# Feed-forward input rows split by GpSimd and transposed by the DMA engines, in place of TensorE

## What is computed

```python
def ffn(x):                                  # k0, k1, k2 are booleans, read as +1 / -1
    h = concatenate([x, -x], -1)
    h = relu(s0 * (h @ sign(k0))) * 2        # 256 -> 512
    h = relu(s1 * (h @ sign(k1))) * 2        # 512 -> 512
    return s2 * (h @ sign(k2))               # 512 -> 128
x = x + 0.5 * ffn(layernorm(x))
x = x + attention(layernorm(x))              # 16 heads of 8; adds its input, then a layernorm with gamma, beta
x = x + 0.5 * ffn(layernorm(x))
```

## Time and profile before

| | before |
|---|---|
| median of 3 runs | 745.43 us |
| profiled execution | 745.53 us |
| its span | 743.7 us |
| outside the span | 1.8 us |
| one full iteration | 42.7 us |
| instructions in the span | 18698 |

### The profile page before, as it was taken

One profiled execution on the slowest core, in us unless ns is written; L12 is line 12 of the kernel. 1 busy time (PEld: TensorE's weight loads), 2 busy tenths in 40 slices (PEclk: granted clock), 3 DMA queues, 4 the chain that ended last, 5 costly groups with the idle time before them and its releaser, 6 DMA issues.

```text
span 743.7 us, 18698 instructions
## 1 busy us (share of the span) xinstructions
PE 695.9 (94%) x7347; PEld 336.0 (45%) x7347; DVE 649.1 (87%) x1270; ACT 510.4 (69%) x745; POOL 365.9 (49%) x650
## 2 busy tenths in 40 slices
PE   7878999999999999999999999999999998787887
PEld 3434344544444454444444444444445444342346
DVE  6687898989999899999989898999989898887766
ACT  3426777777777777777787777767777776766644
POOL 6532455574454647454463746445465745254330
PEclk9999999999999999999999999999999999999999
DMA  3101010201102020201102020110201001010000
GB/s 82 57 15 52 16 53 2 65 17 45 37 3 66 17 66 16 67 17 29 39 16 66 16 66 17 44 38 2 67 17 65 17 33 36 30 38 2 11 7 30
DMA packets 29527, 25.65 MB, mean 34 GB/s; under 512 B 4353, under 2 KB 29441, under 8 KB 29441
## 3 DMA queue, kind: packets, MB, share of 16 engines
q1 hardware_dynamic: 27824, 23.74, 10.0%
q10 hardware_dynamic: 1616, 0.72, 0.3%
HBM read 5.05 MB, written 4.19 MB: 12 GB/s over the span
## 4 chain that ended last, share of the span: by engine, by line
PE 70%; DVE 20%; issue 4%; ACT 3%; POOL 2%; DMA 1%; SPq 0%; DVEq 0%; POOLq 0%
PE ps_c L876 15%; PE ps_z L702 13%; PE ps_z L703 11%; DVE row_max L1507 9%; PE ps_s L823 9%; DVE ffn_lo L1382 6%; PE ps_z L692 3%; PE ps_z L693 3%; PE ps_z L684 2%; PE ps_m L808 2%; PE ps_m L797 2%; ACT ffn_hi L1117 2%; PE ps_c L797 2%; PE ps_z L713 2%; DVE k_lo L1498 1%
## 5 line engine op out<-in xcount | busy, mean ns | idle before, releaser
L1507 DVE TENSOR_REDUCE row_max<-ps_s 128x4 f32<-128x1024 f32 x256 | 312.3, 1220 | 31.0 <-PE ps_s L823 29.3
L1156 ACT ACTIVATE probs<-ps_t,score_scale 128x1024 f32<-128x1024 f32 x252 | 280.2, 1112 | 62.2 <-PE ps_t L836 59.6
L1117 ACT ACTIVATE ffn_hi<-ps_z 128x512 f16<-128x512 f32 x261 | 149.8, 595 | 80.1 <-PE ps_z L703 63.2
L702 PE MATMUL ps_z<-ffn_hi,w 128*128 128x512 f16 x464 | 177.1, 382 | 0.8
L703 PE MATMUL ps_z<-ffn_lo,w 128*128 128x512 f16 x464 | 175.9, 379 | 0.0
L1382 DVE SCALAR_TENSOR_TENSOR ffn_lo<-ps_z,ffn_hi 128x512 f16<-128x512 f32 x232 | 154.3, 684 | 20.3 <-ACT ffn_hi L1117 17.4
L876 PE MATMUL ps_c<-probs,v_cols 128*32 128x256 f32 x2048 | 131.9, 386 | 1.3 <-ACT probs L1156 0.7
L823 PE MATMUL ps_s<-k_rows,q_rows 32*128 32x256 f16 x1024 | 100.2, 273 | 14.8 <-DVE row_max L1507 12.7
L836 PE MATMUL ps_t<-q_rows,k_rows 32*128 32x256 f16 x992 | 97.1, 273 | 0.0
L876 PEld LDWEIGHTS ps_c<-probs,v_cols 128*32 128x32 f32 x2048 | 57.0, 109 | 54.3 <-issue 26.6
L823 PEld LDWEIGHTS ps_s<-k_rows,q_rows 32*128 32x128 f16 x1024 | 29.0, 92 | 103.8 <-issue 50.4
(11 more groups left out here) (223 smaller groups left out, 1101.6 us busy)
## 6 DMA issues: line engine op xcount, KB each, us to landing
x<-L_attn_x SPq DMA_DIRECT2D x16, 256.0 KB, 2.7
q_rows<-q_hi SPq DMA_DIRECT2D x32, 128.0 KB, 2.5
k_rows<-k_hi SPq DMA_DIRECT2D x31, 128.0 KB, 2.1
y<-x SPq DMA_DIRECT2D x15, 256.0 KB, 2.2
q_rows<-no_max SPq DMA_DIRECT2D x16, 128.0 KB, 2.2
q_rows<-q_lo SPq DMA_DIRECT2D x16, 128.0 KB, 2.2
k_rows<-k_lo SPq DMA_DIRECT2D x15, 128.0 KB, 2.1
q_rows<-max_rows SPq DMA_DIRECT2D x64, 8.0 KB
```

The source lines that it names most:

```text
L702: pe.matmul(o[:], w, ffn_hi[:, 1 + k, :], start=(k == 0), stop=False)
L1117: a_.activation(ffn_hi[:, use, :], ps_z[use % 2][:], ACT.Relu if use else ACT.Copy, scale=1.0 if use else XN_SCALE).then_inc(z_hi, 1)
L1156: a_.activation(probs[n % PROBS][:, j:j + 2, :], o[:], ACT.Exp, scale=score_scale[:, 0:1]).then_inc(s_exp, 1)
L1507: v.tensor_reduce(row_max[hb % 2][:].rearrange("p (a l) e -> p l a e", a=2)[:, j:j + 2, :, g % 2], ps_s[:].rearrange("p l (a k) -> p l a k ...
```

## The change

For 26 of the 29 feed-forwards (all but f = 0, 27 and 28, `FFNS_ON_PE`), piece 0 is gone from TensorE, ScalarE and VectorE. In its place GpSimd's new `ffn_rows_norm` scales by 1/deviation times 2^8 (`ffn_rs_fit`, one more 128x4 instruction), writes the scaled rows twice, as f16 into `ffn_rows` (the `hi` part) and as float32 into `ffn_xn`, and subtracts the first from the second into the other half of `ffn_rows` (the `lo` part). SyncE then issues one DMA transpose of the 128 x 1024 f16 rows into `ffn_cols` (`turn_ffn`), and the first input matmul waits for it to land. The two banks are now used nine times for such a feed-forward, so counts and bank numbers follow from helpers (`z_before`, `z_use`, `z_bank`). Three tables change: the statistics of A are taken at steps 2, 2, 5, 5 and its mean at 6 (before 2, 2, 9, 9 and 10); B's mean is taken at step 26 (before 27) and the attention input's at 27 (before 26).

```diff
-AT_STATS_A, AT_STATS_B, AT_STATS_PREP = ((2, 2, 9, 9), 10), ((24, 24, 25, 25), 27), ((18, 18, 20, 20), 26)
+AT_STATS_A, AT_STATS_B, AT_STATS_PREP = ((2, 2, 5, 5), 6), ((24, 24, 25, 25), 26), ((18, 18, 20, 20), 27)
...
+        FFNS_ON_PE = (0, second_ffn(T - 4), second_ffn(T - 3))
...
+            def turn_ffn(f):
+
+                sp.wait_ge(z_full, z_use(f - 1, 5))
+                sp.wait_ge(f_xn, f + 1)
+                sp.dma_start_transpose(ffn_cols[:], ffn_rows[:].rearrange("p i d -> p (i d)")).then_inc(s_cols, 16)
+
             def steps(it):
...
                 if it.cur and it.prev:
                     place_max(t, par, 0)
+                if it.first and it.prev:
+                    turn_ffn(it.next_b)
+                elif it.stats_a and by_dma(it.ffn_a):
+                    turn_ffn(it.ffn_a)
                 if not it.prev:
-                    sp.wait_ge(z_free, Z_USES)
+                    turn_ffn(it.ffn_b)
+                    sp.wait_ge(z_free, z_before(1))
...
                 if it.cur:
                     place_max(t, par, 2)
+                if it.next_b is not None and (not it.first or not it.prev):
+                    turn_ffn(it.next_b)
...
+            g.memset(xn_scale[:], XN_SCALE)
...
+            def ffn_rows_norm(f, src):
+
+                k = rs_steps(f)
+                pool.wait_ge(f_mv, f + 1)
+                g.tensor_tensor(ffn_ve[:], ffn_mv[:, :, 1], eps[:], ALU.add).then_inc(f_rs, 1)
+                g.tensor_tensor(ffn_xc[:], src[:], ffn_mv[:, :, 0:1].broadcast_to([P, TT, P]), ALU.subtract)
+                pool.wait_ge(f_rs, k + 1)
+                g.tensor_tensor(ffn_rs[:], ffn_ve[:], minus_half[:], ALU.pow).then_inc(f_rs, 1)
+                pool.wait_ge(f_rs, k + 2)
+                g.tensor_tensor(ffn_rs_fit[:], ffn_rs[:], xn_scale[:], ALU.mult).then_inc(f_rs, 1)
+                pool.wait_ge(f_rs, k + 3)
+                if by_dma(f - 1):
+                    pool.wait_ge(s_cols, cols_landed(f - 1))
+                else:
+                    pool.wait_ge(z_full, z_use(f - 1, 0) + 1)
+                fit = ffn_rs_fit[:].unsqueeze(2).broadcast_to([P, TT, P])
+                g.tensor_tensor(ffn_rows[:, 0:TT, :], ffn_xc[:], fit, ALU.mult)
+                g.tensor_tensor(ffn_xn[:], ffn_xc[:], fit, ALU.mult).then_inc(f_rs, 1)
+                pool.wait_ge(f_rs, k + 4)
+                g.tensor_tensor(ffn_rows[:, TT:2 * TT, :], ffn_xn[:], ffn_rows[:, 0:TT, :], ALU.subtract).then_inc(f_xn, 1)
...
             def ffn_in(f, m):
...
-                pe.wait_ge(z_free, Z_USES * f + 1 + max(0, m - 1))
-                o = bank_of(1 + m)
-                pe.matmul(o[:], w0[:, m * P:(m + 1) * P], ffn_hi[:, 0, :], start=True, stop=False)
-                pe.matmul(o[:], w0[:, m * P:(m + 1) * P], ffn_lo[:, 0, :], start=False, stop=True).then_inc(z_full, 1)
+                if by_dma(f) and m == 0:
+                    pe.wait_ge(s_cols, cols_landed(f))
+                pe.wait_ge(z_free, z_use(f, 1 + m) - 1 + (m == 0 and not by_dma(f)))
+                o = z_bank(f, 1 + m)
+                pe.matmul(o[:], w0[:, m * P:(m + 1) * P], ffn_cols[:, 0:TT, :], start=True, stop=False)
+                pe.matmul(o[:], w0[:, m * P:(m + 1) * P], ffn_cols[:, TT:2 * TT, :], start=False,
+                          stop=True).then_inc(z_full, 1)
...
             def ffn_piece(f, s):
 
-                if s == 0:
+                if s == 0 and not by_dma(f):
                     ffn_transpose(f)
```

More of the change, by code:

```diff
@@ L188, in macaron_layer @@
         solo_rs = sb("solo_rs", [P, TT])
+        ffn_rs_fit = sb("ffn_rs_fit", [P, TT])
+        ffn_rows = sb("ffn_rows", [P, 2 * TT, P], F16)
+        ffn_cols = sb("ffn_cols", [P, 2 * TT, P], F16)
         ffn_hi = sb("ffn_hi", [P, 9 + KC, TILE], F16)
@@ L308, in macaron_layer, with by_dma, z_before, z_use @@
         assert (LOOP_TO - LOOP_FROM) % 2 == 0 and LOOP_FROM % 2 == 0
+        FFNS_ON_PE = (0, second_ffn(T - 4), second_ffn(T - 3))
+        def by_dma(f):
+            return f not in FFNS_ON_PE
+        def z_before(f):
+            return sum(Z_USES - by_dma(n) for n in range(f))
+        def z_use(f, use):
+            return z_before(f) + use - by_dma(f)
+        def hi_made(f, use):
+            return z_use(f, use) - f + 1
+        def cols_landed(f):
+            return 16 * sum(by_dma(n) for n in range(f + 1))
+        def rs_steps(f):
+            return sum(4 if by_dma(n) else 2 for n in range(f))
+        def z_bank(f, use):
+            return ps_z[z_use(f, use) % 2]
         def run(eng, steps):
@@ L546, in ffn_norm @@
             def ffn_norm(f, src):
-                at_least(pool, z_full, Z_USES * f - (Z_USES - 1))
                 pool.wait_ge(f_mv, f + 1)
-                normalize(ffn_xn[:], src[:], ffn_mv, ffn_xc, ffn_ve, ffn_rs, TT, f_rs, 2 * f, f_xn)
+                normalize(ffn_xn[:], src[:], ffn_mv, ffn_xc, ffn_ve, ffn_rs, TT, f_rs, rs_steps(f), f_xn)
+            def ffn_rows_norm(f, src):
[17 more added lines that the diff above has]
+                g.tensor_tensor(ffn_rows[:, TT:2 * TT, :], ffn_xn[:], ffn_rows[:, 0:TT, :], ALU.subtract).then_inc(f_xn, 1)
             def ffn_deviation(f):
                 pool.wait_ge(f_mv, f + 1)
-                inverse_deviation(ffn_rs, ffn_ve, ffn_mv, TT, f_rs, 2 * f)
+                inverse_deviation(ffn_rs, ffn_ve, ffn_mv, TT, f_rs, rs_steps(f))
             def att_deviation(t):
@@ L680, in ffn_transpose @@
                     pe.wait_ge(q_lo[SOLO_FIRST], 5)
-                at_least(pe, z_free, Z_USES * f - 1)
+                at_least(pe, z_free, z_before(f) - 1)
                 pe.wait_ge(f_xn, f + 1)
                 for i in range(TT):
-                    last = pe.transpose(bank_of(0)[:, i * P:(i + 1) * P], ffn_xn[:, i, :], ident[:])
+                    last = pe.transpose(z_bank(f, 0)[:, i * P:(i + 1) * P], ffn_xn[:, i, :], ident[:])
                 last.then_inc(z_full, 1)
@@ L1114, in z_split @@
             def z_split(f, use):
-                act.wait_ge(z_full, Z_USES * f + use + 1)
-                a_.activation(ffn_hi[:, use, :], ps_z[use % 2][:], ACT.Relu if use else ACT.Copy,
-                              scale=1.0 if use else XN_SCALE).then_inc(z_hi, 1)
+                act.wait_ge(z_full, z_use(f, use) + 1)
+                if use:
+                    a_.activation(ffn_hi[:, use, :], z_bank(f, use)[:], ACT.Relu).then_inc(z_hi, 1)
+                else:
+                    a_.activation(ffn_cols[:, 0:TT, :], z_bank(f, 0)[:].rearrange("p (i n) -> p i n", i=TT), ACT.Copy,
+                                  scale=XN_SCALE).then_inc(z_hi, 1)
             def ffn_piece(f, s):
-                if s == 0:
+                if s == 0 and not by_dma(f):
                     z_split(f, 0)
@@ L1440, in ffn_apply @@
             def ffn_apply(f, src):
-                dve.wait_ge(f_rs, 2 * f + 2)
-                at_least(dve, z_full, Z_USES * f - (Z_USES - 1))
+                dve.wait_ge(f_rs, rs_steps(f) + 2)
+                dve.wait_ge(f_xn, f)
+                if not by_dma(f - 1):
+                    dve.wait_ge(z_full, z_use(f - 1, 0) + 1)
                 scale_rows(ffn_xn, src, ffn_mv, ffn_rs, TT).then_inc(f_xn, 1)
```

57 lines of the change are left out of this document (29 added, 28 removed).

## The result

| | before | after |
|---|---|---|
| median | 744.84 us (4 runs) | 760.20 us (4 runs) |
| from, to | 744.24 to 748.40 | 758.46 to 761.72 |
| profiled execution | 745.53 us | 761.72 us |
| its span | 743.7 us | 759.9 us |
| one full iteration | 42.7 us | 43.8 us |

The ratio is 1.0195, with a 95% interval of 1.0156 to 1.0235: the changed kernel is slower by 1.6 to 2.4%. The forecast was 760.3 us. Its direction and its main mechanism are what happened.

A forecast was written before the change was run, and what follows sets the result against it. The prediction took TensorE, busy 94% of the span, to bound the kernel, with GpSimd also on the path at the iteration boundary. Its sum: 745.5 - 15.3 + 28.1 + 1.8 + 0.2 = 760.3 us, range 746 to 780.

The forecast's parts named there:

- TensorE's transposes, 15.3 us off: Four f32 transposes leave TensorE's path in each of 26 feed-forwards, 0.59 us each: 15.3 us off.
- The series on GpSimd, 5.9 us: GpSimd's instructions making a feed-forward's rows last 5.9 us instead of 3.3, so B ends at 286.1.
- Rival 2: GpSimd's f16 instructions L615 and L618 take about half the time, nothing shifts at the boundary: 730 us, chance 0.1.
- L: Time from issue to landing of the transposing DMA, taken as 3.7 us, the middle between 2.7 and 4.7.
- the sum of packets: Upper bound on L: 1024 pieces as packets, 2.7 us, on top of about 2.0 per transfer: 4.7 us.
- The lower bound: L at least 2.7 us, from the 256 KB load of x and the 128 KB copies inside SBUF.
- L - 1.15: TensorE's stall before B's first input matmul at a boundary, for L above 2.85: forecast 2.55 us.
- the term of 28.1 us: Stall of TensorE at 11 boundaries that hand over a B, 2.55 us each: 28.1 us on.
- The one of iteration 0: Stall of TensorE for B's columns from iteration 0 to 1: 1.8 us on.
- The statistics at steps 5, 5, priced at nothing: VectorE's 0.5 us of statistics moved to step 5 fall where TensorE stands at the boundary anyway: no cost.
- Rival 1: DMA no slower than a copy, L up to 2.85; GpSimd alone stalls the boundary 1.7 us: 749.8 us, chance 0.28.
- Rival 3: Each piece of the DMA is handled twice, L 7.5 us, boundary stall 6.35 us: 806 us, chance 0.12.

The follow-up runs named there:

- A alone: Kernel before with only the inputs A of the twelve second feed-forwards by DMA, A's statistics at steps 7, 7: 739.54 us, ratio 0.9915.
- shorter series: Changed kernel with GpSimd's second multiplication and subtraction for the 11 boundary-crossing B on one block of four: 744.71 us, ratio 0.9982.
- B early: Changed kernel with B's statistics and rows some steps earlier, GpSimd's order changed, A's statistics at steps 4, 4, 7, 7: 732.48 us, ratio 0.9821.
- control: Kernel before with the early-B run's tables and GpSimd order, without transposition by DMA: 746.77 us, ratio 1.0015.

## Why the prediction was right, point by point

**TensorE's transposes, 15.3 us off.** Right. Period by period: 0.64 us less with A alone, 1.23 less with both, where 0.59 and 1.18 were the terms. The 0.05 more may be the room that ScalarE's and VectorE's savings give, which I had counted at nothing; no run tells that apart.

**The series on GpSimd, 5.9 us.** Measured 5.8. The two durations taken from float32 rows were fair: L615, which writes f16, takes 1.04, as L534 in the earlier trace rows; the subtraction 1.16, 0.1 less than L594. Rival 2 (f16 at half the time) has fallen. B was expected 0.3 us earlier by the exchange of the means, to end at 286.1 by the clock of before; it ended at 291.94 - 5.96 = 286.0.

**L and the stall.** The mechanism is as told: TensorE stands before L760, released by a DMA, at 11 boundaries and not before A, as the run with the plain copy (L down by 0.7, wait down by 0.7) and that with the shorter series (1.38 for 1.38) show. The size was off. I put L at 3.7, the middle of its bounds, and it was 3.1, nearer to the plain transfers in the earlier trace rows than to the sum of packets. The price of a packet was what failed. A transposition has 1056 packets where the plain copy has 144 (from the queue's rows, over 26), and these 912 more cost 0.7 us. The 42.8 ns came from packets of 853 bytes on average; by the queue's share of after (14.7% of 759.9 us, against 10.0% of 743.7), one of the new packets took about 22 ns, an estimate. The lower bound was no bound either, since the plain copy of this size landed after 2.4 us. By the formula L - 1.15 the stall should be 1.95; it was 1.77. So the term of 28.1 us is 11 x 1.77 = 19.5 us: 8.6 too much. The one of iteration 0 was 1.0 instead of 1.8.

The Trainium skill's page "Advanced Engine Details and Errata", section X-Bar Transpose (TRN2), has transposing DMAs as fast as plain ones; here the same 256 KB took 3.1 against 2.4 us from issue to landing, so the two aren't equal at this size. The Trainium skill's page "VectorE: DVE Perf Modes", section The three transpose paths, gives 1309 ns for one 128x128 block by DMA. They don't add up over the blocks of one DMA: eight of them landed in 3.1 us.

**The statistics at steps 5, 5, priced at nothing.** This step failed. I had put them into the stretch in which TensorE stands at the boundary. But that stretch ends with L760 at step 2; the statistics come later, and VectorE hands on its maxima at step 8 late. The row of step 8 has 0.41 us of waiting, and the table alone in the kernel before costs 0.47 us a period and 5.8 us in all. The other suspect was that VectorE now waits 1.0 us for the rows `x2` at each boundary. These are its rows in the changed kernel and in the one with A's statistics at 7, 7:

```profile
DVE ffn_bn L1554 <- POOL x L658: 11.4, 12, 1.0
```

```profile
DVE ffn_bn L1554 <- POOL x L658: 11.3, 12, 1.0
```

The second has the same wait for `x2` and none at step 8, and the run with the table alone has the wait at step 8 and none for `x2`. So the late rows cost nothing there. The earlier trace rows had VectorE busy for 39.2 of 42.7 us, and the chain gave it 20%: that was the warning that half a microsecond on it isn't free everywhere.

**The sum again.** With the measured terms: 745.5 - 15.3 + 19.5 + 1.0 + 0.2 = 750.9 us, and 5.8 for the statistics: 756.7. The profiled execution was 761.7. The 5 us that are left match TensorE's clock, which the prediction left out of its sum as granted in full: by the rows in the last section the profiled execution lost 6.8 us to it, where that of before lost 1.7. Only 1.7 of the 5.1 us more stand behind a wait for the DMA. So the sum came out near 760 because 8.6 + 0.8 us too much and 5.8 + 5.1 us too little met.

By period, away from falls of the clock, the account closes to within 0.1 us (waits are those of one row in the middle of the profile):

| kernel | transposes | wait for columns | wait for `att_xn` | wait at step 8 | sum | measured against 42.73 |
|---|---|---|---|---|---|---|
| changed | -1.18 | +1.77 | 0 | +0.41 | +1.00 | +1.08 |
| A's statistics at 7, 7 | -1.18 | +1.77 | 0 | 0 | +0.59 | +0.62 |
| plain copy | -1.18 | +1.03 | +0.34 | +0.27 | +0.46 | +0.51 |
| shorter series | -1.18 | +0.39 | +0.17 | +0.41 | -0.21 | -0.30 |
| statistics 5, 5 in before | 0 | 0 | 0 | +0.41 | +0.41 | +0.47 |
| only A | -0.59 | 0 | 0 | 0 | -0.59 | -0.64 |
| B early | -1.18 | 0 | 0 | 0 | -1.18 | -1.23 |
| control | 0 | 0 | 0 | 0 | 0 | 0.00 |

**Rival 1** (GpSimd alone holds the boundary, about 750) wasn't what happened, but it lies just below: with a plain copy, `att_xn` is waited for at step 6. Its stall was put at 1.7 us and measured 1.4. **Rival 3** (a slow DMA) has fallen with L = 3.1.

## What to carry to other kernels

Work that is taken off the bounding engine is worth its full time only if the new producer's result is there when it is wanted: here the same transposition gave 0.6 us each for A, which has room, and cost more than it gave for B, whose series on two other engines begins 7 us before it is wanted and takes 9. So move the producer's start along with the change, and check it with a control that has the new order alone. On an engine that is busy 90% of a loop, half a microsecond may be free at one step and not at another: VectorE's statistics cost 5.8 us at steps 5, 5, and at steps 7, 7 the wait at step 8 is gone. Every table entry that moves work needs a look at what the engine hands on next.

## What the runs showed of the hardware

**A fall of TensorE's clock costs 1.7 us, and a short wait ahead of it doesn't settle whether it comes.** In stretches of 1 us, the profiled execution of before is below full clock once, and loses 1.7 us by it; that of after loses 6.8 us, in four such portions: two in the head, one behind a boundary, one in the tail. First before, then the head and the tail of after (PE busy is the second number; the clock the last but two):

```profile
679.00:683.00 4.00, 3.80 (x35) 1.08 (x36) 2.51 (x7) 1.50 (x3) 1.38 (x3) 0.57 0.01 2
```

```profile
53.00:61.00 8.00, 6.99 (x33) 2.57 (x30) 4.29 (x6) 2.07 (x4) 1.55 (x4) 0.57 0.01 1
695.00:699.00 4.00, 3.58 (x34) 0.98 (x34) 2.73 (x7) 1.55 (x3) 1.16 (x3) 0.57 0.01 2
```

In the changed kernel the boundary of iterations 12 and 13, with its 1.78 us of standing still up to 601.89, is followed by a stretch at 0.51 of the clock, which is the lower level of 1.2 GHz; in the kernel with matmuls in the wait the same stretch has 1.00. First the changed kernel:

```profile
600.00:603.00 3.00, 1.22 (x13) 0.45 (x12) 1.71 (x3) 1.77 (x3) 2.69 (x8) 1.00 0.73 179
603.00:606.00 3.00, 3.00 (x34) 1.26 (x33) 1.87 (x3) 1.54 (x4) 2.92 (x4) 0.51 0.00 0
```

and with matmuls in the wait:

```profile
600.00:603.00 3.00, 2.86 (x22) 0.98 (x19) 1.64 (x3) 1.71 (x3) 2.69 (x7) 1.00 0.72 175
603.00:606.00 3.00, 3.00 (x46) 1.41 (x46) 2.52 (x4) 2.56 (x5) 2.92 (x5) 1.00 0.01 2
```

The other ten boundaries of the changed kernel have the same wait and no fall in this execution, so the wait alone doesn't bring it; that it helps to is argued from this boundary and the one of 3.11 us, and not shown. In the tail, TensorE has the same two waits of 0.68 and 1.31 us for VectorE's maxima in all ten profiled executions; the clock falls behind them in eight, and not in those with B early and with matmuls in the wait.

The times of one kernel go with its clock, in steps of about 1.5 us. The 17 of the kernel before beside the last four kernels, as medians by mean granted clock: 744.26 us at 1.000 (5 runs), 745.85 at 0.998 (8, which still spread from 745.52 to 747.18), 747.38 at 0.995 (3), 748.25 at 0.993 (1). The changed kernel: 758.46 at 0.995, 760.20 at 0.993 (2 runs), 761.72 at 0.991; that with B early 730.38 at 1.000 (2 runs). At the same clock the change costs 11.1 us (0.995) to 12.0 (0.993), by one run of one of the two kernels each; the rest of its 15.4, 3.4 to 4.3 us, goes with its lower clock. The control falls too, in the head, where the profiled execution of before did not. The same stretch, first of before, then of the control:

```profile
56.00:60.00 4.00, 3.00 (x22) 1.29 (x20) 2.65 (x4) 2.20 (x3) 0.63 (x3) 1.00 0.00 0
```

```profile
56.00:60.00 4.00, 4.00 (x20) 1.83 (x18) 1.08 (x1) 0.81 (x2) 0.62 (x3) 0.58 0.00 0
```

The control has no transposing DMA, and its waits ahead of this stretch are those of before (0.47, 1.06, 0.32, 0.21 and 1.12 us, to 0.01). So a fall in the head doesn't need the change; whether the change makes it likelier stays open. That the filled wait keeps the clock up on the mean stays open, since its runs are too few: 757.50 at 0.998, 758.72 at 0.995 (2 runs), 760.37 at 0.993.

**The transposing DMA.** 3.1 us from issue to landing for 128 x 1024 f16, steady (3.1 to 3.2 in 26 of the changed kernel), and 2.4 us for a plain copy of the same bytes (2.3 to 3.3); 1056 packets against 144. Its issue takes 1.27 us of SyncE's queue in the changed kernel (the plain copy's 0.52), and up to 2.46 with B early. In the other kernels with transpositions the slowest landing took 4.0 to 4.6 us, and 3.7 with matmuls in the wait; what delays these is open.
